# Attention on one core: the heads' reciprocal root mean square as one power on GpSimd, in place of logarithm, exponential and a Newton step

## What is computed

```python
q = (x @ Wq.T + bq) ...; k = ...; v = ...          # 16 heads of 8; two streams of queries and keys
q1, q2, k1, k2 = rope(...)
a1 = softmax(causal(q1 @ k1.T * scale)); a2 = softmax(causal(q2 @ k2.T * scale))
attn = a1 - lam * a2
out = einsum('bhqk,bhkd->bhqd', attn, v)
rms = mean(out * out, axis=-1)                      # over the 8 numbers of a head
out = out * rsqrt(rms + EPS)                        # EPS = 1e-6
out = out * head_norm_w * (1 - LAMBDA_INIT)
return out.reshape(B, S, D) @ Wo.T + bo
```

## Time and profile before

| | |
|---|---|
| median of 3 runs | 1902.27 us (1902.24 to 1903.05) |
| the profiled execution | 1901.86 us, its span 1900.0 us |
| mean granted TensorE clock | 0.976 of full speed |
| busy over the span | PE 90%, DVE 72%, ACT 67%, POOL 55% |
| one full turn of the attention | 29.81 us |
| busy in one such turn | PE 27.58, DVE 23.27, ACT 20.60, POOL 11.22 us |

### The profile page before, as it was taken

The page is one execution under the profiler, slowest core; times in us unless marked ns, Lnnn a source line. Parts: engine busy times, 40 slices in busy tenths (PEclk is TensorE's granted clock), DMA queues, the critical chain, the costliest instruction groups (busy, mean ns, idle before and its releaser), DMA issues. The chain is left out here.

```text
span 1900.0 us, 43151 instructions
## 1 busy us (share of the span) xinstructions
PE 1700.9 (90%) x16448; PEld 1233.5 (65%) x16448; DVE 1368.9 (72%) x3442; ACT 1275.2 (67%) x1613; POOL 1048.1 (55%) x703
## 2 busy tenths in 40 slices
PE   4999999993699999999999999999975599999999
PEld 3778777772456656666666666666643487777787
DVE  5777777765877777777777777777751577777775
ACT  4777777771266676766767666676765577777776
POOL 4888888874333433434334343333411688888885
PEclk9999999996899999999999999999998799999999
DMA  3333333222322323233232322323211223333331
GB/s 111 101 112 112 112 112 101 85 90 80 81 63 78 84 60 92 59 85 82 61 92 58 85 77 68 92 54 89 73 28 51 90 99 111 112 106 107 112 107 62
DMA packets 142434, 163.14 MB, mean 86 GB/s; under 512 B 13218, under 2 KB 124018, under 8 KB 141042
## 3 DMA queue, kind: packets, MB, share of 16 engines
q1 hardware_dynamic: 142228, 160.38, 28.0%
HBM read 91.20 MB, written 14.70 MB: 56 GB/s over the span
## 5 line engine op out<-in xcount | busy, mean ns | idle before, releaser
L1002 ACT ACTIVATE att_prob<-att_ring 128x1024 f32<-128x1024 f32 x384 | 389.1, 1024 | 190.6 <-PE att_ring L1223 185.7
L292 POOL TENSOR_TENSOR ffn_h_low<-ffn_h,ffn_h_high 128x1024 fp32r<-128x1024 f32 x192 | 458.8, 2403 | 95.0 <-ACT ffn_h_high L341 94.8
L1108 DVE TENSOR_REDUCE att_nmax<-att_ring 128x4 f32<-128x1024 f32 (+1 forms) x384 | 454.0, 1218 | 73.0 <-PE att_ring L1223 72.4
L479 DVE TENSOR_TENSOR ffn_h<-ffn_up,ffn_comb_wide 128x1024 f32<-128x1024 f32 x256 | 311.3, 1216 | 125.0 <-ACT ffn_up L334 122.7
L334 ACT ACTIVATE ffn_up<-ffn_up 128x1024 f32<-128x1024 f32 x256 | 258.1, 1008 | 202.8 <-PE ffn_up L567 201.0
L341 ACT ACTIVATE ffn_h_high<-ffn_h 128x1024 fp32r<-128x1024 f32 x256 | 269.3, 1052 | 0.7 <-DVE ffn_h L479 0.7
L918 POOL TENSOR_TENSOR att_qk<-att_turned 128x512 f32<-128x512 f32 x64 | 81.5, 1273 | 321.2 <-DVE att_turned L1087 321.2
L567 PE MATMUL ffn_up<-ffn_xt_high,ffn_w_high 128*128 128x512 f32 x512 | 214.6, 419 | 1.6 <-DVE ffn_h L479 1.5
L580 PE MATMUL ffn_y<-ffn_h_high,ffn_w_high 128*128 128x512 f32 x512 | 205.5, 401 | 7.3 <-POOL ffn_h_low L292 6.0
L284 POOL TENSOR_TENSOR ffn_ez<-ffn_e_const,ffn_nz 128x16 f32<-128x16 f32 x64 | 185.8, 2904 | 38.2 <-DVE ffn_nz L405 38.2
L567 PE MATMUL ffn_up<-ffn_xt_low,ffn_w_high 128*128 128x512 f32 x512 | 203.5, 397 | 0.0
(11 more groups left out here) (142 smaller groups left out, 2826.8 us busy)
## 6 DMA issues: line engine op xcount, KB each, us to landing
ffn_comb_wide<-ffn_comb_d SPq DMA_DIRECT2D x128, 512.0 KB, 5.6
att_qs<-att_parts SPq DMA_DIRECT2D x192, 128.0 KB, 2.5
att_kd<-att_parts SPq DMA_DIRECT2D x192, 128.0 KB, 2.5
ffn_x<-x SPq DMA_DIRECT2D x32, 256.0 KB, 3.1
ffn_w<-w SPq DMA_DIRECT2D x4, 1024.0 KB, 7.2
x<-ffn_out SPq DMA_DIRECT2D x16, 256.0 KB, 2.4
att_x<-x SPq DMA_DIRECT2D x32, 128.0 KB, 2.3
att_xr<-x SPq DMA_DIRECT2D x32, 128.0 KB, 2.3
```

The costliest lines, as they stand in the source:

```text
L292: nc.gpsimd.tensor_tensor(hts[1][:, e % NH], h[:, e % NH], hts[0][:, e % NH], ALU.subtract).then_inc(low_by_pool, 1)
L479: nc.vector.tensor_tensor(h[:, e % NH], up[:, e % NUP], comb_wide[:, b.c % NW, e].unsqueeze(1).to_broadcast([P, HE, FT]), ALU.mult).then_i ...
L1002: nc.scalar.activation(prob[:, u % NP], ring[:, ORDER.index((kind, u)) % 3], ACT.Exp, scale=SCALE).then_inc(prob_ready, 1)
L1108: nc.vector.tensor_reduce(nmax[:, b, :, h0:h0 + cnt], ring[:, pos % 3] .rearrange("p (s h k) -> p s h k", s=2, k=width), AX.X, ALU.max, ne ...
```

## The change

The logarithm and the exponential on ACT and the four operations of `newton` on DVE go. In their place GpSimd computes `rrms` by one TENSOR_TENSOR with the operation pow, `ms_eps` (128x32) to the power of a tile that holds -0.5. It stands in GpSimd's queue after the unit T 7, behind `rotate 1`. It waits for `ms_eps`, and `scaled` now waits for it. The warm-up logarithm at the start of the attention goes as well, and the tile `minus_halves` is set once.

```diff
-    "streams": ("T", 4), "ms": ("XT", 0), "rms": ("T", 6), "newton": ("S", 1), "scaled": ("T", 0),
+    "streams": ("T", 4), "ms": ("XT", 0), "rms": ("T", 7), "scaled": ("T", 0),
...
-        NORM = 11
+        NORM = 7
...
+                def rms(turn):
+                    wait(pool, norm_step, turn.at(-3, NORM, NORM))
+                    wait(pool, pool_norm, turn.at(-4, 5, 3))
+                    nc.gpsimd.tensor_tensor(rrms[:], ms_eps[:], minus_halves[:], ALU.pow).then_inc(rrms_ready, 1)
+
                 def scaled(turn):
-                    wait(pool, norm_step, turn.at(-3, NORM, NORM))
+                    wait(pool, rrms_ready, turn.at(-3, 1, 1))
...
+                nc.gpsimd.memset(minus_halves[:], -0.5).then_inc(minus_set, 1)
+                pool.wait_ge(minus_set, 1)
...
+                        if (kind, u) == AFTER["rms"] and turn.runs(-3):
+                            rms(turn)
...
-                act.wait_ge(dve_setup, 2)
-                nc.scalar.activation(ln_ms[:], y0[:], ACT.Ln).then_inc(lam_ready, 1)
...
-                        if (kind, u) == AFTER["rms"] and turn.runs(-3):
-                            wait(act, norm_step, turn.at(-3, NORM, 7))
-                            nc.scalar.activation(ln_ms[:], ms_eps[:], ACT.Ln).then_inc(rms_step, 1)
-                            wait(act, rms_step, turn.at(-3, 2, 1))
-                            nc.scalar.activation(y0[:], ln_ms[:], ACT.Exp, scale=-0.5).then_inc(rms_step, 1)
...
-                        if (kind, u) == AFTER["newton"] and turn.runs(-3):
-                            wait(dve, rms_step, turn.at(-3, 2, 2))
-                            norm(nc.vector.tensor_tensor(newton[:], ms_eps[:], y0[:], ALU.mult), -3, 8)
-                            norm(nc.vector.tensor_tensor(newton2[:], newton[:], y0[:], ALU.mult), -3, 9)
-                            norm(nc.vector.tensor_scalar(newton[:], newton2[:], -0.5, 1.5, ALU.mult, ALU.add), -3, 10)
-                            nc.vector.tensor_tensor(rrms[:], newton[:], y0[:], ALU.mult).then_inc(norm_step, 1)
```

More of the change, by code:

```diff
@@ L759, in attention @@
         ms_eps = sb("ms_eps", [P, QB * H])
[L760 to L763, removed]
+        minus_halves = sb("minus_halves", [P, QB * H])
         rrms = sb("rrms", [P, QB * H])
@@ L780, in attention @@
         v_set = sem("v_set")
+        minus_set = sem("minus_set")
         lam_ready = sem("lam_ready")
@@ L784, in attention @@
         ms_ready = sem("ms_ready")
+        rrms_ready = sem("rrms_ready")
         x_in_s = [sem(f"x_in{k}") for k in range(NSLOT)]
@@ L804, in attention @@
         norm_step = sem("norm_step")
-        rms_step = sem("rms_step")
         pool_norm = sem("pool_norm")
-        NORM = 11
+        NORM = 7
         def wait_unit(engine, turn, kind, n):
@@ L977, in _ @@
                 clear_queries(2)
-                pool.wait_ge(dve_setup, 3)
+                pool.wait_ge(dve_setup, 2)
                 pool.wait_ge(weights_in, 16 * 12)
@@ L1045, in _ @@
                 nc.vector.memset(one_rows[:], 1.0).then_inc(dve_setup, 1)
-                nc.vector.memset(y0[:], 1.0).then_inc(dve_setup, 1)
                 dve.wait_ge(setup, 2)
@@ L1182, in _ @@
                 nc.vector.tensor_scalar(norm_w[:], norm_w[:], 1.0 - LAMBDA_INIT, None, ALU.mult).then_inc(lam_step, 1)
-                dve.wait_ge(lam_ready, 2)
+                dve.wait_ge(lam_ready, 1)
                 nc.vector.scalar_tensor_tensor(out=stream_w[:, :, 1], in0=by_head(1), scalar=-LAMBDA_INIT,
@@ L1194, in _ @@
             def _(te):
-                te.wait_ge(dve_setup, 3)
+                te.wait_ge(dve_setup, 2)
                 te.wait_ge(v_set, 1)
```

## The result

The changed kernel takes 1917.82 us (median; 1917.48 to 1917.92), the kernel before 1902.26 (1901.6 to 1903.05): 0.79% slower, ratio 1.0079 with a 95% interval from 1.0063 to 1.0094. The prediction said 1918.5 us, from 1908 to 1931. The profiled execution has a span of 1916.0 us where before had 1900.0.

The account below looks back on a forecast made before the run. The steady turn was taken as one chain through PE with short visits to DVE and ACT. Full turns +21.2 and last turns -5.0 gave +16.2 us, so 1918.5 us against the median, range 1908 to 1931.

Parts of the forecast that it names:

- The power's cost: On GpSimd, the 128x32 power was to take 5.43 us, extended from widths 2, 4 and 16; bounds 5.3 and 5.8.
- Nothing gained by the removal in a full turn: Taking 3 us from ACT and 1 us from DVE was to gain a full turn nothing.
- The control taken from turn 2: Turn 2, without head norm, takes 13.76 us from T 6 to T 11; the full turn takes 13.75.
- The path through `left 0`, `mid 0`, T 10 and T 11: Power delays `left 0` on GpSimd; ACT waits 2.3 us at `mid 0`, T 0 is 0.75 us late, period about 30.56.
- S 6 and T 0: On PE, S 6 waits 0.2 us for T 10's buffer, and T 0 idles some 0.5 us for ACT's exponential.
- The last turns: From turn 31 on: -4.4 us in turn 31, -1.8 and -1.5 in turns 32 and 33, +2.7 in 34; sum -5.0.
- The start: Removing one table load and one small operation from ACT, adding a GpSimd memset: 0, within 0.2 us either way.
- A larger delay with a price in clock: Rival: costlier power, later transfers or lost clock before T 0 cost 1.0 to 1.3 us a turn; chance 0.12.
- the fourth rival: The delay is larger, 1.0 to 1.3 us a turn, giving 1923 to 1934 us; chance 0.12.

Follow-up runs that it names:

- run 1: The changed kernel with the power taken out too, so no logarithm, exponential, Newton step or head normalisation; 1890.66 us, ratio 0.9943.
- run 2: The kernel before, keeping logarithm, exponential and `newton`, with the same power added in the same place and its result unread; 1926.36 us, ratio 1.013.
- run 4: The changed kernel with the power over 48 columns instead of 32, the last 16 never read; 2022.57 us, ratio 1.0633.

## Why the prediction was right, step by step

- *The power's cost.* Taken at 5.43 us from three widths, measured at 5.441. With the runs the line now has six points; the last three, 4.175, 5.441 and 8.032 us at 24, 32 and 48 columns, give 158 and 162 ns a column. The rate of the Trainium skill (GPSIMD Engine Reference, 3.1 Elementwise) for a two-input operation, which the prediction did not go by, would have made 32 columns about 70 ns, an estimate; by the line here they are 5.06 us, some 70 times as much.
- *Nothing gained by the removal in a full turn.* Shown by run 1, whose turn is 29.80 us. The control taken from turn 2 had said the same.
- *The path through `left 0`, `mid 0`, T 10 and T 11.* ACT waits 2.23 us (said: 2.3). From `mid 0` on the distances are 0.53, 0.90 and 0.52 us, where the prediction's times have 0.5, 1.0 and 0.5. The period is 30.56, as said.
- *S 6 and T 0.* Behind the weighing that precedes it, S 6 starts after 1.64 us (932.15 to 933.79), before after 1.44: the 0.2 that was forecast. From S 6 to T 0 it is 1.43 us against 0.89, 0.54 more, where some 0.5 was forecast; the bracket calls 0.38 of it idle. Together they are the 0.75.
- *The last turns.* Turn 31: -4.4 forecast, -4.40 measured, from T 6 to T 8 on ACT (9.25 before, 4.85 after), and PE's wait of 3.47 us is 0.38. The next two turns: -1.8 and -1.5 forecast, -1.73 and -1.46 measured. Turn 34: +2.7 forecast, +2.81 measured:

```profile
1468.00 0.18 DVE L1134 TENSOR_SCALAR att_ms_eps<-att_ms 128x32 f32<-128x32 f32 x1
1468.26 5.44 POOL L940 TENSOR_TENSOR att_rrms<-att_ms_eps,att_minus_halves 128x32 f32<-128x32 f32 x1 [0.75 <-DVE att_ms_eps L1134]
1473.77 0.63 POOL L945 TENSOR_TENSOR att_o_n<-att_o,att_rrms 128x256 f32<-128x256 f32 x1
```

- *The start.* Put at 0 within 0.2 us, it was +0.43. This is a mis-sized term. It arises in PE's first two blocks of QK products: they take 5.64 and 6.25 us where before they took 5.26 and 6.05, at a granted clock of 0.65 and 0.58 against 0.70 and 0.61. Why the clock is lower there is open; in run 1 the blocks take 5.22 and 6.04 us. The first block, before, then after:

```profile
454.48 5.26 PE L1223 MATMUL att_ring<-att_xt,att_wqk 128*128 128x256 f32 x16 [2.72 <-ACT att_xt L996]
...
454.38 5.64 PE L1216 MATMUL att_ring<-att_xt,att_wqk 128*128 128x256 f32 x16 [2.71 <-ACT att_xt L1003]
```

- *A term that was missing.* Behind turn 33 the kernel before ran at a low clock, and the changed one does not. That is -1.00 us, which the sum didn't hold. PE's last two weighings, first before, in one row at a clock of 0.71, then after, at 1.00 (timeline and window of each):

```profile
1445.02 4.00 PE L1238 MATMUL att_o_ps<-att_prob,att_v 128*32 128x256 f32 x64
...
1444.00:1449.80 5.80, 5.02 (x77) 2.53 (x70) 0.00 (x0) 3.66 (x5) 0.00 (x0) 0.71 0.01 3
```

```profile
1458.67 1.51 PE L1231 MATMUL att_o_ps<-att_prob,att_v 128*32 128x256 f32 x32
1460.60 1.51 PE L1231 MATMUL att_o_ps<-att_prob,att_v 128*32 128x256 f32 x32 [0.42 <-ACT att_prob L1009]
...
1458.00:1463.00 5.00, 3.77 (x79) 2.16 (x76) 0.00 (x0) 3.63 (x5) 0.00 (x0) 1.00 0.00 0
```

What keeps the clock up is open. PE's wait of 2.59 us ahead of T 9 of turn 33 is 1.12 in the changed kernel. But that doesn't explain it: run 2 has this wait, and its clock stays up as well.

```profile
1466.08 0.39 PE L1238 MATMUL att_ring<-att_qs,att_kd 64*128 64x256 bf16 x4 [2.58 <-ACT att_prob L1016]
...
1466.08:1472.00 5.92, 4.69 (x93) 2.98 (x94) 0.00 (x0) 3.94 (x5) 0.72 (x2) 1.00 0.00 0
```

The missing term, the start and the last stage together are -0.46 us, the other terms +0.26 above theirs: 16.0 us of span where 16.2 were forecast.

- *The rivals.* A larger delay with a price in clock was given 0.12. It did not come at 5.44 us, but it is real: run 4 shows it behind gaps of 2.7 us.
- *Two slips in the sums.* 28 x 0.75 is 21.0, and the sum takes 21.2; the measured 21.24 is that of turns 0.76 longer. And a delay of 1.0 us a turn gives 1925 us, not the 1923 at which the fourth rival begins.

## What to carry to other kernels

The busy share of an engine says how much work it can take in, not where. Before work is moved to the idlest engine, find who waits on that engine's queue behind the new place, and give it an idle stretch that ends before the result is wanted: here that is worth 21 us (1917.82 to 1896.72), with the same work. When an operation is moved, look also at what its followers are pushed beside, since a GpSimd addition that slides next to a small VectorE operation can hold it until it ends.

## What was unexpected of the hardware

- A VectorE operation on 2 columns took 0.88 us instead of 0.17 beside a 128x512 addition on GpSimd, and one on 32 columns 0.58 instead of 0.19 beside a 128x256 addition. Beside a power on GpSimd the first kept its 0.17, and a product of two 128x32 tiles its 0.18. An add that reads PSUM was not held.
- The power's time on GpSimd is in the columns: 152 to 162 ns for each, from 2 to 48, on all 128 partitions.
- A gap of 2.72 us on PE in the midst of a turn at full clock was followed by 4.39 us at 0.62 of it; gaps of half a microsecond were not. Yet one of 2.85 us in the kernel before and one of 2.58 in run 2 were followed by a full clock.
